# Query tiles 8 to 15 of an attention stage spread over every second group, the odd tile of a pair scaled half a beat later

## What is computed

```
# block 3: attention over 32 heads of 16, queries and keys normalised by head
q = x @ Wq.T ; k = _rmsnorm(context @ Wk') ; v = context @ Wv'
q = _rmsnorm(q)
scores = jnp.einsum('bhnd,bhmd->bhnm', q, k) * scale
out = jnp.einsum('bhnm,bhmd->bhnd', softmax(scores), v)
x = x + tanh(g) * out
# block 4: for each token, the best of 64 tiles by the signs of its normalised row
best_cluster = argmax(sign(xn) @ cluster_sigs.T)
tile_idx = argmax(where(in_cluster, sign(xn) @ tile_sigs.T, -inf))
x = x + tanh(g) * (spline of that tile on its 8 features)
```

## Time and profile before

| | |
|---|---|
| median of three runs | 1187.44 us (1183.65, 1187.44, 1187.78) |
| span of the profiled execution | 1172.7 us |
| median less span | 14.7 us |
| attention stage, first to last group | about 827 to 1124 us of the span |
| busy over the span | PE 84%, DVE 60%, ACT 57%, POOL 43% |

### The profile page before, as it was taken

One profiled execution on the slowest core, in us unless ns is written; L12 is line 12 of the kernel. 1 busy time (PEld: TensorE's weight loads), 2 busy tenths in 40 slices (PEclk: granted clock), 3 DMA queues, 4 the chain that ended last, 5 costly groups with the idle time before them and its releaser, 6 DMA issues. The chain is left out here.

```text
span 1172.7 us, 27955 instructions
## 1 busy us (share of the span) xinstructions
PE 990.9 (84%) x9515; PEld 567.5 (48%) x9516; DVE 705.2 (60%) x1724; ACT 672.1 (57%) x1091; POOL 504.0 (43%) x442
## 2 busy tenths in 40 slices
PE   5888989968999978899999999955899888888740
PEld 2545556445677656677777777742122211111120
DVE  8676755578888457322223222216688787877687
ACT  4655545445544267444445444435777789899950
POOL 0222232156676265555556555532233343433422
PEclk9999999998999989999999999987899999999975
DMA  6534231389985496766666666648598687497211
GB/s 234 178 127 138 82 129 62 130 194 229 227 209 138 132 370 155 148 122 112 120 146 117 116 117 117 119 68 219 134 178 172 154 187 145 102 180 147 65 42 64
DMA packets 183494, 170.87 MB, mean 146 GB/s; under 512 B 137173, under 2 KB 138773, under 8 KB 182485
## 3 DMA queue, kind: packets, MB, share of 16 engines
q1 hardware_dynamic: 155554, 111.62, 36.9%
q0 software_dynamic: 25888, 56.43, 24.1%
q10 hardware_dynamic: 1954, 1.54, 0.4%
HBM read 80.82 MB, written 65.20 MB: 125 GB/s over the span
## 5 line engine op out<-in xcount | busy, mean ns | idle before, releaser
L2020 ACT ACTIVATE sb_atp<-ps_atpS 128x1024 f32<-128x1024 f32 x256 | 242.6, 1037 | 40.5 <-PE ps_atpS L1759 40.5
L1444 PEld LDWEIGHTS ps_shpH<-sb_roxT,sb_rowt 128*128 (+1 forms) x2844 | 170.3, 107 | 20.7 <-DVE sb_roxT L1311 1.8
L1444 PE MATMUL ps_shpH<-sb_roxT,sb_rowt 128*128 128x128 f16 (+1 forms) x2844 | 174.7, 221 | 1.6 <-DVE sb_roxT L1311 1.6
L1433 PE MATMUL ps_shpY<-sb_rowt,sb_rohhl 128*128 (+1 forms) x711 | 170.4, 386 | 3.3 <-DVE sb_rowt L1324 2.9
L1771 PE MATMUL ps_atpO<-sb_atp,sb_atv 128*17 128x512 f32 x1024 | 137.3, 609 | 34.0 <-ACT sb_atp L2020 28.7
L1167 ACT ACTIVATE sb_roh<-ps_shpH,sb_rob 128x128 f32<-128x128 f32 (+1 forms) x237 | 68.8, 361 | 103.5 <-PE ps_shpH L1444 100.6
L1070 POOL DMA_INDIRECT sb_roxg<-xn,sb_roentry x79 | 85.1, 1077 | 87.9 <-DMA sb_roentry<-list 62.0
L1433 PEld LDWEIGHTS ps_shpY<-sb_rowt,sb_rohhl 128*128 128x128 f16 (+1 forms) x711 | 67.4, 99 | 71.6 <-issue 7.8
L1156 ACT ACTIVATE sb_roy<-ps_shpY,sb_roentry 128x512 f32<-128x512 f32 x79 | 54.2, 686 | 78.6 <-PE ps_shpY L1433 75.0
L1058 POOL DMA_INDIRECT list<-sb_shentry,sb_shposb x64 | 74.0, 1157 | 33.5 <-DVE sb_shposb L1239 18.5
L1077 POOL DMA_INDIRECT x2a<-sb_roy,sb_roentry x40 | 65.5, 1637 | 44.2 <-ACT sb_roy L1156 41.8
(11 more groups left out here) (355 smaller groups left out, 1771.5 us busy)
## 6 DMA issues: line engine op xcount, KB each, us to landing
sb_rowt<-rw SPq DMA_DIRECT2D x15, 768.0 KB, 9.6
sb_rowt<-rw SPq DMA_DIRECT2D x15, 704.0 KB, 6.5
kst<-sb_kykp SPq DMA_DIRECT2D x16, 512.0 KB, 3.5
qst<-sb_quqp SPq DMA_DIRECT2D x12, 512.0 KB, 4.0
vst<-sb_kyvt SPq DMA_DIRECT2D x16, 272.0 KB
sb_atv<-vst SPq DMA_DIRECT2D x32, 136.0 KB, 3.9
sb_stage<-ctxT SPq DMA_DIRECT2D x4, 1024.0 KB, 7.4
sb_shxin<-x SPq DMA_DIRECT2D x16, 256.0 KB, 5.4
```

The source lines that it names most:

```text
L1433: last = e.matmul(pY[it.p][:, :], hhl[it.p][0:n, x, k * P:(k + 1) * P], weight(value, 2 * W1 + w + k * D, n, D), start=j == 0, stop=j == l ...
L1444: last = e.matmul(rpH[it.p][0:n, f * P:(f + 1) * P], weight(ex["up"], w + k * FF + f * P, P, n), rxT[it.p][:, x + k, :], start=j % (3 * KD ...
L2020: S.done(e.activation(pr[n % 6][:, :], pS[n % 3][:, :], ACT.Exp, scale=HD ** -0.5 / SA ** 2), "atexp")
```

## The change

Two lines change: the slots of query tiles 9 to 15, and the beat at which the second tile of a pair is scaled and split.

```diff
-        q_slot = [-16, -15, -14, -13, -4, -2, 0, 2, 4, 6, 8, 10, 12, 14, 26, 30]
+        q_slot = [-16, -15, -14, -13, -4, -2, 0, 2, 4, 8, 12, 16, 20, 24, 28, 32]
         c_slot = [17, 21, 25, 29, 33, 37, 41, 45, 49, 52, 55, 58]
         n_slot = {i: q_slot[i] + 8 for i in range(5, NT, 2)}
...
             for i, at in n_slot.items():
-                out_ += [It((i - 1 + j) // 2, j) for j in range(2) if at + lag == h]
+                out_ += [It((i - 1 + j) // 2, j) for j in range(2) if at + lag + (j if i > 2 * FIRST else 0) == h]
```

## The result

| | before | after |
|---|---|---|
| median | 1188.51 us (14 runs, 1183.65 to 1194.88) | 1183.26 us (14 runs, 1177.52 to 1193.40) |
| ratio, 95% interval | | 0.9952 [0.9931, 0.9972] |
| span of the profiled execution | 1172.7 us | 1180.1 us |
| group 3 to group 22 | 181.56 us | 175.40 us |
| first turn of a group | 842.46 us | 855.88 us |

What follows compares the result with a forecast made beforehand. The exponentials on ScalarE bound a free group; groups 3 to 22 held 12.83 us of waits. Striking these and adding 8.75 of new ones gave 4.1 us less, from 1187.44 to 1183.3 us, range 1176 to 1191.

Steps and rivals of the forecast that it cites:

- The likeliest case: Groups 3 to 22: 12.83 us of waits go, 8.75 of new ones come, 4.1 us less; chance 0.50.
- sum of new waits: Groups 9 to 22: 1.1 + 3.5 + 3.5 + 0.65 = 8.75 us of waits added by the change.
- What is removed: Groups 3 to 22: late projection copies, late `sb_law` and the lower clock behind it go, 12.83 us in all.
- 9 to 10: Group 9: VectorE's work of beat 18 carries 1.4 us over, so the sign comes 1.1 us late.
- 12 to 13 and 16 to 17: Groups 12 and 16: `roots` and `inner` delay the projection 1.0 us, and 0.8 is paid at its copy; 1.8 each.
- 13 to 14 and 17 to 18: Groups 13 and 17: VectorE carries 2.0 us in from the beat before, so the sign is 1.7 us late.
- 21 to 22: Group 21: VectorE carries 3.1 us in, and its sum of 6.2 makes a wait of 0.65 us.
- "slower" rival: Groups 9, 13, 17, 21: GpSimd late for `scales`, signs late and clock lower; 10.4 us more, 1197.8; chance 0.11.
- The loads, costed at nothing: SyncE's queue: transposing loads come more than 5 us ahead of the projection and are costed at nothing.
- "Absorbed": Sign and projection start also have a free 1.0 us; 3.1 of 8.75 left, 9.7 us less, 1177.7; chance 0.22.
- "Locked": Groups 11, 15, 19: `roots` waits about 1.4 us for L1919; 4.2 us more, 1187.5, no change; chance 0.17 (locked or moved).

Runs made afterwards that it cites:

- all pairs apart: The changed kernel with the second tile scaled later for the pairs of tiles 4 to 7 too; 1186.48 us beside 1187.43 for the kernel before.
- the half beat alone: The changed kernel with its query slots put back, keeping the later scaling of a pair's second tile; 1176.57 us beside 1177.77 for the kernel before, ratio 0.9985.
- the slots alone: The changed kernel with both tiles of a pair scaled in the same beat again; 1174.01 us beside 1177.77 for the kernel before, ratio 0.9959.
- a gap behind tile 13: The changed kernel with tiles 9 to 11 at old slots, 12 and 13 at 16 and 20; 1186.92 us beside 1192.75 for the kernel before, ratio 0.9960.
- the packed one: The changed kernel with tiles 9 to 11 at old slots and every pair's second tile scaled later; 1178.15 us beside 1185.80 for the kernel before, ratio 0.9933.

## Why the prediction was right, and where its steps were off

The time predicted, 1183.3 us, is the measured median to 0.1 us. That much is luck: 4.1 us less were predicted from 1187.44, and 5.3 less were measured from 1188.51; in the windows it was 6.16. The likeliest case is the one that happened, the late waits go and smaller ones come; its sum of new waits, 8.75, was 2.1 too high. By its own terms:

- *What is removed.* Right for 5 to 6, 7 to 8, 11 to 12 and 19 to 20, which are at 7.66 or 8.17 in the table. For 3 to 4 it was wrong by a mis-sized term: `low` took the 1.45 that it was given, but `squares` was taken at 1.5 and took 2.36, as its L2133 too stretches to 1.52 beside the second cast, so that 0.37 stayed. With one cast there (all pairs apart) it is gone. The 1.22 of lower clock behind group 11 was struck rightly for the trace of before, but it is not there in every execution, so it was not wholly the change's to win. And of 9 to 10 I had the reason wrong: ahead of TensorE's wait of 0.82 stood a late `normalise`, not a late copy alone.
- *9 to 10*, 1.1 predicted, 0.45 measured. `parts` paid no 0.8 for the cast, so beat 18 ended 0.63 into group 9 instead of 1.4, ahead of where `normalise` starts anyway (0.76): nothing was carried over. `low` took 0.6 instead of 1.0. What is left comes from a term that the sum did not have, `squares` stretched by 0.4 beside GpSimd's copy L1911.
- *12 to 13 and 16 to 17*, 1.8 predicted, 1.55 measured. The chain was as worked out: `roots` 2.79 long, `inner` ending 2.37 into the group instead of 2.45, an idle gap of 1.06 ahead of the projection and one of 0.73 behind the copy.
- *13 to 14 and 17 to 18*, 1.7 predicted, 0.73 measured. This is the step that failed. The end of beat 26 was put 2.0 us into group 13; it was 1.14. `parts` was charged 0.8 for its partner's cast, and took 0.68 beside it, while the cast took 1.44 (1.03 at 961.49, with no such neighbour); the other 0.35 of the 1.2 by which beat 26 ended sooner after its turn is that of the copy, at T + 8.05 instead of 8.4. With one Newton step the sign is as late as ever: the carry is set by what stands behind the copy, not by `roots`. What the sum had right is that a late sign is paid: 0.77 late cost 0.73.
- *21 to 22*, 0.65 predicted, 1.19 measured, by another path. VectorE itself was ready 1.61 before L1915 on GpSimd was. That is the "slower" rival's chain, at one sign instead of four, without the lower clock in this execution; it starts from VectorE's late scaling, so that `roots` sets it in the end (8.35, 9.36 and 10.39 with one, three and five steps).
- Not in the sum at all: 0.06 at 18 to 19 and 0.04 at 6 to 7. The loads, costed at nothing, cost next to nothing in the changed kernel, but not in its neighbours: 2.51 for `sb_atq` with the half beat alone, 1.76 for the gather with the slots alone.

*The rivals.* "Absorbed" is excluded as a mechanism: its total of 1177.7 supposed a free microsecond at the sign and at the projection's start, but from one step to five each microsecond of `roots` was paid in full in group 12, and so were all but 0.04 of the 0.77 at the sign of group 13. "Locked" falls for the place it named: `roots` took 954.60 to 957.39, 2.79 us as before, with L1919 running until 956.04, and its instructions 0.23 each. The Trainium skill, SBUF — State Buffer, section "SBUF: two separate sides", says that of an instruction of VectorE with two SBUF inputs and one of GpSimd that reads SBUF, the one that starts first gets the shared port pair and the other is fully blocked; L1919 had started first. The trace disagrees for `roots`. It does not clear L1919 altogether: with a gap behind tile 13, L2157, with two inputs too, took 1.10 instead of 0.68 beside it. Why one is stretched and the other not stays open. Beside the casts the rows do agree with such a rule: L2133 took 1.52 beside them, and L2167, which had started 0.14 us ahead of a cast, took its 0.68 while the cast took 1.44. No experiment here changed which of the two starts first. "Slower" is real but needs more than this change does: in group 13 L1915 had 0.53 us to spare, not the 1.6 of the prediction; its wait shows at 21 to 22, and with 1.03 us in the kernel with a gap behind tile 13.

Left open: why the part ahead of the stage differs between chips, and what decides whether the clock falls behind a wait.

## What to carry to other kernels

When an order is moved by hand, list for each event that another engine waits for (here the sign and the projection) what stands ahead of it on its engine within two beats, and price the move there; work that comes behind the event costs only what it carries over to the next one. Follow it through the other engines too: `roots` on VectorE made a sign late by way of GpSimd's queue. Read such a change in windows between two fixed points of the trace, never in the span: here the effect was 6 us, and the unchanged part ahead of it differed by up to 22, mostly from chip to chip. A sum of windows needs its clock read beside it: two executions of the kernel before agreed in the sum, and not in its parts. And before a schedule is spread evenly, try moving only the pieces that stand ahead of an event: with only the last four tiles moved the windows were 0.6 us shorter, in one execution, than with the whole change.

## What the hardware did that was not expected

- The granted clock after a wait. Behind the same group of 10.8 us (TensorE idle 3.37 and 3.36) it was 0.81 in one execution and 1.00 in another (8.88 and 7.67 us); behind the same 9.36 it was 1.00 in the changed kernel and 0.81 in the packed one. Within the kernel with the half beat alone, it was 1.00 behind 2.73 us of idle time (group 11) and 0.81 behind 2.20 (group 19), so that the longer wait did not decide it.
- Casts on GpSimd stretched VectorE's instructions with two inputs: L2133 from 0.68 to 1.52, L2210 from 0.74 to 1.60, L2209, of one column, from 0.21 to 0.87. The copy L1911 does it too (L2133 from 0.69 to 1.10). L1919, which is longer than a cast, left `roots` alone, but stretched L2157 from 0.68 to 1.10 in the kernel with a gap, and L2116, with one full-size input, from 0.55 to 0.81 in the kernel before (at 967.17).
- A gather becomes visible when the beats get short: `inner` waited 1.76 us for it in the kernel with the slots alone. So does the transposed load of the queries, with 2.51 us in the kernel with the half beat alone.
